# A state-space input phase on one core: raw dt, the turning of x, and the softplus arguments move across a batch boundary

## What is computed

```python
x_in = (x @ in_proj_w.T)[..., :512]
x_in = silu(depthwise_causal_conv(x_in, conv_w) + conv_b)      # this is u, 512 channels
x_dbl = x_in @ x_proj_w.T                                      # dt_raw (1), Bp (16), Cp (16)
dt = softplus(dt_raw @ dt_proj_w.T + dt_proj_b)                # 512 channels a token
dt = clip(dt, 1e-4, 10.0)
```

## Time and profile before

| what | us |
|---|---|
| three timed runs: median (lowest to highest) | 5886.45 (5882.94 to 5886.98) |
| the profiled execution: its time | 5887.31 |
| the profiled execution: its span | 5885.6 |
| busy over the span: PE, DVE, ACT, POOL | 4821.2, 4835.5, 3731.3, 1092.2 |
| weights of the input phase start to load | 3250.66 |
| first convolution of the loop (batch 1) starts | 3311.83 |
| last subtraction of the phase starts | 3885.99 |

### The profile page before, as it was taken

The page is one execution under the profiler, slowest core; times in us unless marked ns, Lnnn a source line. Parts: engine busy times, 40 slices in busy tenths (PEclk is TensorE's granted clock), DMA queues, the critical chain, the costliest instruction groups (busy, mean ns, idle before and its releaser), DMA issues. The chain is left out here.

```text
span 5885.6 us, 94545 instructions
## 1 busy us (share of the span) xinstructions
PE 4821.2 (82%) x27420; PEld 2058.2 (35%) x27420; DVE 4835.5 (82%) x10599; ACT 3731.3 (63%) x5401; POOL 1092.2 (19%) x1593
## 2 busy tenths in 40 slices
PE   6979798988979797959998544438888888878878
PEld 3343434334433434326665222201111111115555
DVE  6777777868686877758887688879999999988868
ACT  5656656556666565634444577768888888875533
POOL 0000010101000000001111000024444444435511
PEclk8989899998989898979999766655555555559989
DMA  0000000000000000001111333331111111125522
GB/s 26 1 8 8 9 8 9 8 9 8 1 16 1 16 1 8 1 31 37 43 41 39 98 126 123 116 100 50 50 48 49 50 50 50 49 68 177 175 76 71
DMA packets 198911, 273.62 MB, mean 46 GB/s; under 512 B 13989, under 2 KB 157989, under 8 KB 192454
## 3 DMA queue, kind: packets, MB, share of 16 engines
q1 hardware_dynamic: 181190, 252.90, 13.6%
q10 hardware_dynamic: 17408, 16.78, 0.8%
HBM read 151.14 MB, written 118.49 MB: 46 GB/s over the span
## 5 line engine op out<-in xcount | busy, mean ns | idle before, releaser
L714 DVE TENSOR_REDUCE at_nmax<-at_ps_t 128x1 f32<-128x512 f32 x2048 | 1337.4, 686 | 347.2 <-PE at_ps_t L366 334.1
L538 ACT ACTIVATE at_probsT<-at_ps_s 128x1024 f32<-128x1024 f32 x1024 | 992.3, 1021 | 616.9 <-PE at_ps_s L398 616.9
L366 PE MATMUL at_ps_t<-at_qkT 108*128 108x512 bf16 x2048 | 819.9, 402 | 38.3 <-DVE at_nmax L714 22.3
L2124 DVE SCALAR_TENSOR_TENSOR sc_decayed<-sc_da,sc_state 128x256 f32<-128x256 f32 x2048 | 775.5, 424 | 9.0 <-ACT sc_da L2079 8.0
L2086 ACT ACTIVATE sc_xd<-sc_ps_du,sc_bt 128x512 f32<-128x512 f32 x1024 | 650.8, 693 | 176.5 <-PE sc_ps_du L2027 176.5
L2134 DVE CUSTOM_DVE_ANT_0 sc_state<-sc_xd,sc_decayed 128x256 f32<-128x256 f32 x2048 | 759.0, 412 | 0.0
L1992 POOL TENSOR_SCALAR sc_xd<-sc_xd 128x1024 f32<-128x1024 f32 x512 | 532.2, 1040 | 804.4 <-ACT sc_xd L2086 804.4
L2016 PE MATMUL sc_da<-sc_parts,sc_sel 24*128 24x512 bf16 x1024 | 566.4, 609 | 120.2 <-DMA sc_sel<-sc_sel 84.2
L2027 PE MATMUL sc_ps_du<-sc_parts,sc_sel 24*128 24x512 bf16 x1024 | 565.1, 609 | 112.3 <-ACT sc_xd L2086 112.3
L388 PE MATMUL at_ps_s<-at_qkT 108*128 108x512 bf16 x2048 | 616.5, 384 | 15.0 <-ACT at_probsT L538 11.7
L2079 ACT ACTIVATE sc_da<-sc_da,sc_a_col 128x1024 f32<-128x1024 f32 x512 | 563.7, 1101 | 0.4 <-PE sc_da L2016 0.4
(11 more groups left out here) (316 smaller groups left out, 7682.8 us busy)
## 6 DMA issues: line engine op xcount, KB each, us to landing
dt_parts<-si_pt SPq DMA_DIRECT2D x64, 384.0 KB, 2.6
du_parts<-si_pu SPq DMA_DIRECT2D x64, 384.0 KB, 3.2
sc_parts<-dt_parts SPq DMA_DIRECT2D x128, 192.0 KB
sc_parts<-du_parts SPq DMA_DIRECT2D x128, 192.0 KB
u_tok<-si_ut SPq DMA_DIRECT2D x8, 2048.0 KB, 8.3
y<-sc_yo SPq DMA_DIRECT2D x256, 64.0 KB
so_yin<-y SPq DMA_DIRECT2D x32, 512.0 KB
so_uin<-u_tok SPq DMA_DIRECT2D x32, 512.0 KB
```

Of the source, the lines that this page charges most:

```text
L366: nc.tensor.matmul(ps_t[c][:], qkT[0:KP, hd, t * P:(t + 1) * P], qkT[0:KP, H + hd, c * HALF:(c + 1) * HALF], start=True, stop=True).then_i ...
L538: nc.scalar.activation(probsT[:, c % RING, :], ps_s[c % 2][:], ACT.Exp).then_inc(s_exp, 1)
L714: nc.vector.tensor_reduce(nmax[:, par, c, t:t + 1], ps_t[c][:], AX_X, ALU.max, negate=True).then_inc(s_max, 1)
L2124: nc.vector.scalar_tensor_tensor(decayed[:, ch], da[q % 2][:, j % 2, ch], DECAY_MIN, state[:, (j - 1) % SRING, ch], ALU.max, ALU.mult).the ...
```

## The change

- On DVE, `rests` and `third_parts` of a tile come one step later in `tokens` (step t does `rests(t-2)` and `third_parts(t-3)`), so three tiles of products stand ahead of the first `rests` instead of two.
- `dt_taken` of the next batch moves from the head of DVE's loop turn into step 6 of `tokens`; `arguments` moves from the head of the turn to the place ahead of the last `third_parts`. For batch 0 both stand ahead of the loop, and behind the loop they are gone.
- ACT's `x_stored` of the next batch moves from the head of the loop turn to its end, behind the last `u_stored`; `second_parts` of tile 7 goes behind it. The last turn is written out behind the loop.
- PE's first batch is written out ahead of its loop. The wait for all eight u tiles ahead of the projection becomes one wait for each of the first four outputs.
- SP's program is the same.

```diff
 # PE
-            with pe.Fori(0, B) as b:
+            def batch(b, first):
                 pe.wait_ge(s_x, b * 16 + 16)
-                pe.wait_ge(s_dtraw, b)
+                if not first:
+                    pe.wait_ge(s_dtraw, b)
...
                 pe.wait_ge(s_xT, 4 * b + 4)
-                pe.wait_ge(s_uts, b * TB)
                 for m in range(KI):
                     for hf in range(NHALF):
                         n = m * NHALF + hf
+                        if n < 4 and not first:
+                            pe.wait_ge(s_uts, b * TB + n - 3)
...
+            batch(0, True)
+            with pe.Fori(1, B) as b:
+                batch(b, False)
 # ACT
-            with act.Fori(1, B) as b:
-                x_stored(b)
+            x_stored(1)
+
+            def batch(b, more):
                 for m in range(KI):
...
                     if t >= 3:
                         u_stored(b, t - 3)
-                second_parts(b - 1, TB - 1)
                 for t in range(TB - 3, TB):
                     u_stored(b, t)
+                if more:
+                    x_stored(b + 1)
+                second_parts(b - 1, TB - 1)
+
+            with act.Fori(1, B - 1) as b:
+                batch(b, True)
+            batch(B - 1, False)
 # DVE
-            def tokens(b):
+            def tokens(b, more):
...
                     if t < TB:
                         products(b, t)
-                    if t <= TB:
-                        rests(b, t - 1)
                     if t >= 2:
-                        third_parts(b, t - 2)
+                        rests(b, t - 2)
+                    if t >= 3:
+                        third_parts(b, t - 3)
+                    if t == TB - 2 and more:
+                        dt_taken(b + 1)
+                if more:
+                    arguments()
+                third_parts(b, TB - 1)
 
             conv(0)
+            dt_taken(0)
+            arguments()
             with dve.Fori(1, B) as b:
-                dt_taken(b - 1)
-                arguments()
                 conv(b)
-                tokens(b - 1)
-            dt_taken(B - 1)
-            arguments()
-            tokens(B - 1)
+                tokens(b - 1, True)
+            tokens(B - 1, False)
```

## The result

The changed kernel takes 5836.24 us (median of 4 runs, 5833.93 to 5838.37) against 5886.15 us (5882.94 to 5886.98): a ratio of 0.9915, 95% interval 0.9903 to 0.9926. That is 49.9 us, or 0.85%, faster. The forecast was 5846 in a range of 5833 to 5859, with faster at 0.91.

A forecast was written before the change was run, and what follows sets the result against it. DVE was taken to bound the input phase, idle 8.56 us of a 75.29 us turn. Turns of 68.87 gain 36.4 us, the phase's end 4.0: 40.4 off 5887.31 is 5846.9, less 0.86 for timed runs 5846, range 5833 to 5859.

The forecast's parts named there:

- the two waits: DVE idling each turn: 2.37 us at tile 0 for ACT's rounded parts, taken as gone; 5.28 at the batch boundary, 1.2 left.
- The x chain: From step 7 through ACT's copies and PE's turning of x to the projection at 62.65 us and the convolution at 68.87.
- The uncertain term: PE's clock as a projection starts: 6.22 us from there to the convolution, bounds 4.36 and 8.25.
- the sum: Six turns of 68.87 us gain 36.4, the end of the phase 4.0; together 40.4 off the profiled 5887.31, so 5846.9.
- The end of the phase: After convolution 7 the last arguments start 3.6 us earlier and 0.47 of "issue" ahead of them falls away: 4.0.
- 52.03 + 15.60 = 67.63: DVE's step 7 start after the convolution plus what it does from there: when DVE is ready for the next convolution, in us.
- the rival of a full clock: Rival: the projection starts at 2.4 GHz on PE, a turn of 67.0 us, 51.6 saved, 5835 us; chance 0.20.
- New waits inside the steps: Rival: ACT's casts and DVE's subtractions interlock; 6 us of new idling a turn leaves no gain, about 5886 us; chance 0.06.
- the ring: Rival: with four slots, stores taking over 12.0 us stop DVE; slower by 0.2% at 18.5 us, 5898 us; chance 0.03.

The follow-up runs named there:

- e1: The changed kernel with `rests` and `third_parts` back one step earlier, where they stood before the change; 5863.02 us.
- e4: The kernel before with only `rests` and `third_parts` one step later, raw dt, turning of x and arguments left at the batch boundary; 5859.27 us.
- e7: The changed kernel with raw dt copied just ahead of the arguments instead of in step 6; 5857.06 us.
- e3: The changed kernel with ACT's x copies behind the second parts of tile 7, these ahead of the last three u copies; 5852.41 us.
- e5: The changed kernel with six unread transposes added on PE between the turning of x and the projection; 5827.31 us.
- e2: The changed kernel with the eight arguments behind the last third parts instead of ahead of them; 5840.94 us.
- e8: The changed kernel run again with nothing altered; 5836.03 us, ratio 0.9927 against the kernel before, timed beside it.
- e9: The kernel before, order untouched, with three unread transposes added on PE between the turning of x and the projection; 5877.59 us.
- e6: The changed kernel with raw dt in step 5, x turned ahead of the last u tile and copied ahead of the last three u copies; 5840.54 us.

## Why the prediction was right, point by point

**Where the time went.** Right. It named the two waits, and both fell as worked out: 2.37 to nothing, 5.28 to 0.68 (forecast 1.2). e1, e4 and e7 show that each of the two moves is worth 20 to 23 us of the stretch, in e4 with 5.5 us of PE's clock in it.

**The x chain.** Right in each link. After convolution 5 step 7 starts at 51.93 (forecast 52.03), the second parts of tile 5 at 54.44 (54.56), `u_stored` of tile 3 at 55.57 (55.69), the last u tile at 56.20 (56.32), the x copies at 60.03 (60.37), the projection at 62.25 (62.65). That ACT's queue sets it, not PE, was right too: PE idles 1.52 us for the copies, and e3 moves the time by ACT's order alone, with the second parts of tile 7 ahead of the copies.

**The uncertain term.** The bounds held: 4.36 to 8.25 were given from the start of a projection to the convolution, and 5.85 to 7.40 occur where DVE waits for it. The 7.40 is batch 2, with both outputs at 1.2 GHz. In batch 3 the clock was up and DVE ready last. The forecast took 6.22. The gain from convolution 1 to 7 was 40.6 instead of 36.4. Against the 68.87 of the sum, turn 1 took 69.66, turns 2 and 3, on either side of the convolution of batch 3, 67.45 and 67.25, and turns 4 to 6 some 68.2: 0.65 less, 0.4 of it from the chain and 0.25 from the clock. That the mean came so near 68.87 has some luck in it, since the clock went both ways. The Trainium skill's sentence that in one kernel the full clock did not come on in transposes (TensorE: Matmul & The Clock Gate, Part 4: PE-mode transpose) doesn't hold here: in batch 3, with nothing but transposes on PE, it rose (0.64), as it did in batch 2 of the earlier trace rows.

**The end of the phase.** 4.0 forecast, 4.03 measured, and by the way it named: the last arguments start 60.95 us after convolution 7 instead of 64.99, with no "issue" ahead of them.

**The step that was mis-sized.** "It is ready for the next convolution at 52.03 + 15.60 = 67.63" takes along the waits of 0.32 and 0.59 that happened in the turn before, as if they were work. They last only while ACT is the later of the two. DVE's own work is 66.5 (e5), so the floor lies 1.1 us lower, 0.9 of it these two waits. It did no harm to the forecast, since the x chain was later in most turns, but it is why e2 was expected 10 us too slow and e5 4 us too slow, and why the rival of a full clock was put at turns of 67.0 instead of 66.5.

**The rivals.** The median came out beside the time of the full-clock rival, 5835, but not by its mechanism: in five of the six turns DVE still waits for a projection that starts at 1.2 GHz. Of the 9.6 us between the profile and the sum 4.2 are in these turns; the rest is the 4.6 us of the later phases and the 0.8 ahead of the phase, which the sum did not have and which e8's timing does not confirm as a gain. New waits inside the steps didn't come: the wait of DVE on ACT's rounded parts is nowhere in the table of waits of the changed kernel. Nor did the ring bind: ACT's first parts wait 2.3 us in all, for DVE.

## What to carry to other kernels

At a batch boundary, look for the small instruction on which the next batch's first stage hangs; here a copy of 0.16 us at the end of a loop turn held PE, ACT and DVE in a row, and moving it paid in the main only together with the copies that follow on another engine's queue. When reckoning when an engine will be ready, count its work and not the waits it happened to have in the old order: they move with whoever is late. And when two chains are within a us of each other, the level of PE's clock at the start of a burst decides which is later; filling the idle gap ahead of it with useless transposes beat starting the chain earlier.

## What the runs showed that I had not expected

Filling a gap of 0.76 us (e9) or 1.5 us (e5) on PE made the projection behind it start at or near 2.4 GHz in every batch (e5: 1.00 from its start; e9: 1.00 in batch 4, 0.86 over the first 2.1 us in batch 3), and gained 1.4 to 2.2 us in each of turns 2 to 6 in e9 and 9.0 us over six turns in e5; with a gap of 3.7 us (e6) the clock stayed at 1.2 GHz for over 5 us of the projection. But the length of the gap alone does not set it: behind the same 1.52 us the projection starts at 2.4 GHz in batches 2 to 7 of e2 and at 1.2 GHz in batches 2 and 4 to 7 of the changed kernel, and in e2 the clock rose while PE stood idle. The pattern over the batches came out the same in both executions of the changed kernel. And a change of 2.4 us in the length of a turn (e4) switched the clock at the start of three projections out of six, worth 1.7 to 2.1 us each: a saving can be larger or smaller than its own length through the place where it lets the clock rise.
